# Experts of a mixed attention and expert layer: the gathered rows are turned by VectorE instead of TensorE, and the down product is accumulated in one bank region

## The reference, cut to what matters

```python
logits = jnp.einsum('bsd,de->bse', x, gate_w)            # 8 experts
affinity = jax.nn.softmax(logits, axis=-1)
gating, index = jax.lax.top_k(jnp.transpose(affinity, (0, 2, 1)), K)   # K = 256 rows of each batch
x_sel = x[b_idx, index]
g = jnp.einsum('bekd,edi->beki', x_sel, Wg)              # 256 -> 512
u = jnp.einsum('bekd,edi->beki', x_sel, Wu)
h = jax.nn.silu(g) * u
out = jnp.einsum('beki,eid->bekd', h, Wd)                # 512 -> 256
contrib = out * gating[..., None]
x_out = jnp.zeros_like(x).at[b_idx, index].add(contrib)
```

## Time and profile before

| | us |
|---|---|
| median of 3 runs | 1691.63 (1690.6 to 1692.41) |
| profiled execution, its own time | 1691.12 |
| its span, first to last instruction | 1689.2 |
| TensorE busy | 1643.0 (97%) |
| VectorE busy | 1046.5 (62%) |
| ScalarE busy | 1243.3 (74%) |
| POOL busy | 520.2 (31%) |

### The profile page before, as it was taken

The page is one execution under the profiler, slowest core; times in us unless marked ns, Lnnn a source line. Parts: engine busy times, 40 slices in busy tenths (PEclk is TensorE's granted clock), DMA queues, the critical chain, the costliest instruction groups (busy, mean ns, idle before and its releaser), DMA issues.

```text
span 1689.2 us, 27913 instructions
## 1 busy us (share of the span) xinstructions
PE 1643.0 (97%) x10616; PEld 926.4 (55%) x10616; DVE 1046.5 (62%) x2126; ACT 1243.3 (74%) x1544; POOL 520.2 (31%) x480
## 2 busy tenths in 40 slices
PE   6799999999999999999999999999999999999997
PEld 5234344344434434434434433368888888888886
DVE  9774566576575666567657668866555555555543
ACT  5798998998998899899899899954444444444443
POOL 3121121111211111112112100046666565656653
PEclk9799999999999999999999999999999999999999
DMA  5645753764684585476366366155443443534332
GB/s 186 162 104 118 155 134 69 182 136 108 149 173 110 122 177 133 107 161 160 95 151 162 86 146 130 40 162 112 86 95 65 94 95 64 100 63 96 67 56 33
DMA packets 113982, 196.00 MB, mean 116 GB/s; under 512 B 20896, under 2 KB 59680, under 8 KB 113696
## 3 DMA queue, kind: packets, MB, share of 16 engines
q1 hardware_dynamic: 83696, 143.01, 36.0%
q0 software_dynamic: 29040, 49.83, 15.3%
q10 hardware_dynamic: 1088, 1.05, 0.2%
HBM read 117.27 MB, written 76.55 MB: 115 GB/s over the span
## 4 chain that ended last, share of the span: by engine, by line
PE 87%; ACT 6%; DVE 3%; issue 2%; DMA 1%; POOL 1%; POOLq 0%; ACTq 0%; DVEq 0%
PE o_ps L1086 25%; PE score L1170 21%; PE score L1072 17%; ACT probs L854 6%; PE side L956 5%; PE score L1181 3%; PE side L966 3%; PE side L997 3%; PE o_ps L1181 2%; PE score L1183 2%; PE side L1181 2%; PE score L1157 2%; PE o_ps L1183 1%; PE side L1183 1%; PE side L936 1%
## 5 line engine op out<-in xcount | busy, mean ns | idle before, releaser
L854 ACT ACTIVATE probs<-score 128x1024 f32<-128x1024 f32 x1024 | 964.0, 1053 | 94.8 <-PE score L1072 88.8
L1086 PE MATMUL o_ps<-probs,v_ones 128*32 128x512 f32 x4096 | 514.7, 604 | 0.6
L1072 PE MATMUL score<-q_stack,k_stack 50*128 50x512 f32 x2048 | 377.1, 449 | 9.8 <-issue 4.4
L1072 PEld LDWEIGHTS score<-q_stack,k_stack 50*128 50x128 f32 x2048 | 166.4, 185 | 337.3 <-ACT probs L854 302.1
L752 POOL DMA_INDIRECT out<-probs,rot x128 | 212.3, 1659 | 191.7 <-DVE probs L1527 162.5
L833 ACT ACTIVATE probs<-score 128x512 f32<-128x512 f32 x128 | 76.6, 598 | 187.3 <-PE score L1170 187.3
L1086 PEld LDWEIGHTS o_ps<-probs,v_ones 128*32 128x32 f32 x4096 | 97.2, 108 | 210.8 <-issue 147.9
L1513 DVE TENSOR_TENSOR probs<-score,probs 128x512 f32<-128x512 f32 x128 | 88.5, 692 | 180.6 <-PE score L1170 176.3
L730 POOL TENSOR_TENSOR square<-qk 128x512 bf16<-128x512 f32 x56 | 71.0, 1298 | 345.3 <-DVE qk L1368 345.3
L741 POOL DMA_INDIRECT qk<-xn_rows,rot x128 | 135.1, 1055 | 38.3 <-issue 29.2
L1170 PE MATMUL score<-k_stack,zn_hi 128*128 128x512 f32 x512 | 140.1, 390 | 0.0
(11 more groups left out here) (271 smaller groups left out, 2348.3 us busy)
## 6 DMA issues: line engine op xcount, KB each, us to landing
q_parts<-parts SPq DMA_DIRECT2D x16, 1024.0 KB, 5.1
k_parts<-parts SPq DMA_DIRECT2D x16, 1024.0 KB, 8.4
q_stack<-q_parts SPq DMA_DIRECT2D x62, 256.0 KB, 6.2
k_stack<-k_parts SPq DMA_DIRECT2D x62, 256.0 KB, 7.9
q_stack<-q_parts SPq DMA_DIRECT2D x66, 128.0 KB, 6.2
k_stack<-k_parts SPq DMA_DIRECT2D x66, 128.0 KB, 6.7
o_sums<-o_sb SPq DMA_DIRECT2D x256, 32.0 KB
num<-o_sums SPq DMA_DIRECT2D x32, 256.0 KB
```

Of the source, the lines that this page charges most:

```text
L854: act.activation(probs[probs_of(b, s)][:, 2 * i:2 * i + 2, :], score[ring_of(b, p)][:, :, :], ACT.Exp, scale=SCALE).then_inc(exp_done, 1)
L1072: last = pe.matmul(score[ring_of(b, p)][:, w, :], k_stack[par][rows, i, kt * P:(kt + 1) * P], q_stack[par][rows, i, qh * HALF:(qh + 1) * H ...
L1086: last = pe.matmul(o_ps[j * KEYS_W:(j + 1) * KEYS_W, :], v_ones[par][:, kt, j, :], probs[probs_of(b, s)][:, j, :], start=kt == 0, stop=kt ...
```

## The change

1. Rows are turned on VectorE. `turn_rows(unit, a)` takes 32 of the 128 partitions of `xs` and writes, with four STREAM_TRANSPOSE of 32 partitions by 256 elements, one 32-row group of each tile to `x_turned`, a buffer in `cos_sb` that the experts don't use otherwise. Each of the four goes to another group of 32 partitions. Sixteen turn a unit: eight at the end of a unit for the unit after the next, four behind h(0) and four behind h(1) of the next unit. For unit 1, sixteen stand behind h(0) and h(1) of unit 0. TensorE keeps the eight transposes of the first unit alone (`turn_first`).
2. `turned` casts and subtracts 128x1024 at once, from SBUF, instead of twice 128x512 from PSUM.
3. `down` has three 256-wide matmuls for each t and f, all into one 256-column region; tiles 2 and 3 use the freed `xt_ps` banks instead of those of gate and up. For all four tiles first f = 0 and 1, then f = 2, then f = 3. ScalarE's scaling alone makes y; VectorE's (L1527) goes.
4. ScalarE's casts of weights stand before its scalings.
5. The four output projections run in units 1 and 2 between `gate_up` and `down`, instead of at the end of units 0 and 1, and VectorE's part of them stands before the last `low`.
6. POOL's gather waits until the rows of two units before are turned by VectorE (`rows_turned`), instead of by TensorE.

```diff
-        return (d_ps[0], d_ps[1], g_ps[(FC - 1) % 2], u_ps[(FC - 1) % 2])[t]
+        return (d_ps[0], d_ps[1], xt_ps[0], xt_ps[1])[t]
...
-    END_BANKS = {("wo", q): (q // 2, q % 2) for q in range(QUARTERS)}
+    END_BANKS = {("wo", q): (q // 2 + 1, q % 2 + 2) for q in range(QUARTERS)}
...
-            need(pool, xt_full, DC * (unit - 1))
+            if unit == 2:
+                pool.wait_ge(xt_full, DC)
+            elif unit > 2:
+                pool.wait_ge(rows_turned, unit - 2)
...
+            else:
+                act.wait_ge(rows_turned, unit)
+                act.wait_ge(up_full, FC * unit)
+                act.copy(x_hi[:, :, :], x_turned).then_inc(x_high, 1)
...
+            if bp < WEIGHTS and e + 1 < E:
+                high_weights(e + 1, bp)
             need(act, scattered[(bp - 2) % UNITS], ST * DMA * (e + (bp >= 2)))
             for t in range(ST):
                 act.wait_ge(down_full, ST * unit + t + 1)
-                act.activation(y[unit % 2][t], rows_ps(t)[:, D:2 * D], ACT.Copy,
+                act.activation(y[unit % 2][t], rows_ps(t)[:, 0:D], ACT.Copy,
...
-                    pe.matmul(rows_ps(t).rearrange("p (k n) -> p k n", k=2), h_hi[:, f, at], wd_both[k][:, :, f, :],
-                              start=f == 0, stop=False)
-                    last = pe.matmul(rows_ps(t)[:, 0:D], h_lo[f][:, at], we_hi[k][DOWN][:, f, :],
-                                     start=False, stop=f == FC - 1)
+                    for i, (ht, wt) in enumerate(((h_hi[:, f, at], we_hi), (h_lo[f][:, at], we_hi), (h_hi[:, f, at], we_lo))):
+                        last = pe.matmul(rows_ps(t)[:, 0:D], ht, wt[k][DOWN][:, f, :],
+                                         start=i == 0 and f == 0, stop=i == 2 and f == FC - 1)
...
             gate_up(unit)
-            if unit + 1 < E * UNITS:
-                turn(unit + 1)
+            for job in END_JOBS:
+                if END_BANKS[job][0] == unit:
+                    pe.wait_ge(y_scaled, ST * (unit - 1) + END_BANKS[job][1] + 1)
+                    run_job(end_jobs, job, None, NB - 1, rows_ps(END_BANKS[job][1]))
...
+        def turn_rows(unit, a):
+            if unit >= E * UNITS:
+                return
+            if a == 0:
+                dve.wait_ge(gathered[unit % 2], ST * DMA * (unit // 2 + 1))
+                dve.wait_ge(x_split, splits_of(unit - 1))
+            rows = slice(a * BLOCK, (a + 1) * BLOCK)
+            from_rows = xs[unit % 2][rows, :, :].rearrange("p t (c q n) -> p q c t n", c=DC, n=BLOCK)
+            to_cols = x_turned.rearrange("p c (t a k) -> p a c t k", t=ST, k=BLOCK)
+            for q in range(BLOCKS):
+                last = dve.transpose(to_cols[q * BLOCK:(q + 1) * BLOCK, a, :, :, :], from_rows[:, q, :, :, :])
+            if a == BLOCKS - 1:
+                last.then_inc(rows_turned, 1)
...
                 dve.tensor_tensor(h[f % 2], u_ps[f % 2], silu[f % 2], ALU.mult).then_inc(h_done, 1)
+                if unit == 0 and f < BLOCKS // 2:
+                    turn_rows(1, 2 * f)
+                    turn_rows(1, 2 * f + 1)
+                elif f < BLOCKS // 2:
+                    turn_rows(unit + 1, f + BLOCKS // 2)
                 if f > 0:
                     low(unit, f - 1)
...
             if bp < WEIGHTS and e + 1 < E:
                 low_weights(e + 1, bp)
+            turn_rows(unit + 2, 0)
+            turn_rows(unit + 2, 1)
```

## The result

| | before | after |
|---|---|---|
| median, us | 1691.63 (7 runs, 1690.41 to 1699.89) | 1677.72 (7 runs, 1676.23 to 1683.78) |
| profiled execution, its own time | 1691.12 | 1677.62 |
| its span | 1689.2 | 1675.8 |

The ratio is 0.9916, with a 95% interval of 0.9902 to 0.9931. The change makes the kernel faster, by some 14 us or 0.8%; I had said 22.6 (1668.5), with 1664 to 1685 as the range.

A forecast was written before the change was run, and what follows sets the result against it. TensorE's instruction list was taken as the bound. 28 units shorter by 0.954 us give 26.7 us, less 4.1 at the start is 22.6, so 1691.12 becomes 1668.5 us; range 1664 to 1685.

The forecast's parts named there:

- What bounds the kernel, and VectorE hidden: Steady units: TensorE's instruction list sets the time; VectorE's sixteen transposes cost nothing, with 1.0 us to spare.
- chain: VectorE's work in a steady unit with a weight, beside the transposes: 8.2 us, to which sixteen transposes are added.
- The price of the unseen form: A 32x256 STREAM_TRANSPOSE on VectorE, in no row of before: 0.45 us each without overlap, 7.2 us a unit.
- 48 x 0.114 = 5.47 us, against 5.64: TensorE's `down` in each unit: 48 256-wide matmuls at 0.114 us take 5.47 us, where before it took 5.64.
- the 26.7: Gain in us over 28 units, each 0.954 us shorter on TensorE without the eight transposes and with `down` at 5.47.
- The far end of 0.124: Slowest pace allowed for `down`, 0.124 us a 256-wide matmul: `down` 5.95 us, gain 0.47 a unit, 13 us.
- The start costs 4.1 us: First three units: transposes behind the last batch's work on VectorE make TensorE wait, so unit 3 starts 4.1 us later.
- "Cost nothing" of the casts of weights: ScalarE's casts of weights, moved ahead of its scalings, end at 14.6 us, before the first scaling is due: no cost.
- The gathers: POOL's rows for the unit three ahead land at 15.3 to 16.2 us, level with VectorE's need at 14.8 or 16.0.
- The slow `down` (1682): Rival: matmuls of `down` take 0.124 us, not 0.114, so 9 us less in all, 1682 us; chance 0.08.
- VectorE as the bound: Rival: transposes at 0.634 us make VectorE set steady units, 1718 us; chance 0.15, of which 0.12 slower.
- late gathers: Rival: POOL's scatters and gathers come late, 0.6 us a unit lost, between 1673 and 1685 us; chance 0.11.

The follow-up runs named there:

- experiments 3 and 4: The kernel after with two, and with four, further transposes a unit on VectorE into a spare buffer: 1679.43 us and 1695.55 us.
- experiment 8: The kernel after with each 32x256 transpose on VectorE cut into two of 32x128: 1677.92 us.
- Experiment 6: The kernel before with only `down` changed to three 256-wide matmuls and ScalarE's scaling alone, TensorE still transposing: 1693.48 us.
- experiment 7: The kernel after with the three products of `down` ordered high x high, high x low, low x high: 1675.34 us.
- experiment 9: The kernel after once more, unchanged, five executions: 1679.18 us, ratio to before 0.992.
- Experiment 2: The kernel after with the rows of units 1, 2 and 3 turned by TensorE instead of VectorE: 1667.97 us.
- experiment 5: The kernel after with rows of units 1 to 3 turned by TensorE and the silu table loaded early: 1665.50 us; run again, ratio to before 0.9845.
- Experiment 11: The kernel after with ScalarE's casts of weights put back behind its scalings: 1723.95 us.
- experiments 1 to 4 and 11: The first of these is the kernel after with the rows of unit 1 alone turned by TensorE: 1673.32 us; the others have their own lines.

## Why the prediction was right, and where it fell short

The mechanism was right and the time was in the range, but the gain was 14 us and not 22.6. Two terms of the sum were mis-sized, the pace of `down` (4.3 us) and the start (5.7 us); the 0.85 us by which the first `gate_up` came sooner is no merit of either kernel.

- **What bounds the kernel, and VectorE hidden: right.** TensorE's list bounded steady units before and does after. No wait of TensorE from 1200 to 1600 us; VectorE is busy 13.9 us of a unit (14 said); chain 8.35 us (8.2 said) and 1.05 us to spare (1.0 said), by experiments 3 and 4.
- **The price of the unseen form: right.** 0.45 us was put together from other rows; it is 0.436 long and 0.447 apart. That no overlap was counted is borne out by these rows and by the distance between pairs in experiment 8.
- **"48 x 0.114 = 5.47 us, against 5.64": mis-sized.** `down` takes 5.65, 0.1177 a matmul. I took the pace from one projection in unit 1. The same projection in unit 0, time line of PE of the kernel before, starts its pairs 0.235 apart, 0.1175 a matmul:

```profile
1132.97 0.40 PE L997 MATMUL score<-w_hi,at_lo 128*128 128x256 f32 x2
1133.21 0.40 PE L997 MATMUL score<-w_lo,at_hi 128*128 128x256 f32 x2
1133.44 0.40 PE L997 MATMUL score<-w_hi,at_hi 128*128 128x256 f32 x2
```

  Experiment 6 shows the narrow form as a loss of 0.095 us a unit by itself, and the transposes as a gain of 0.896. Together 0.801, 4.3 us less in all than the 26.7. The time lines of the kernel before have 32 such projections of 12 matmuls: behind their first pair 20 of them run at 0.118 and 12 at 0.113 to 0.115. So the form has two paces, I had read one of the quicker ones, and every steady `down` of after runs at the slower one. What sets the pace is open: the DMA share was 0.00 in both stretches, so traffic is not it, and the order of the products makes no difference to `down` (experiment 7). The far end of 0.124 had the late first matmul in it; without these 0.08 us it is 0.120.
- **"The start costs 4.1 us": right in place and mechanism, too small in size.** It cost 9.8 (7.5 in experiment 9's trace of the same kernel). Unit 0 took 23.29 us where 19.35 was worked out: h(0) started 7.2 us behind the first `gate_up`, not 3.7 as before, since the silu table was loaded late, and the transposes queued behind it pushed h(1) and the low parts. Experiment 7, with the early table, has 19.78: so the arithmetic of unit 0 held, and what failed in after is its first step, that h(0) is done when it was in the kernel before (1119.35). Unit 1 took 24.83 where 23.25 was worked out: TensorE's wait (3.5; 4.0 said) was followed by a lower clock, which the sum had at nothing and which cost some 1.7 us (an estimate from the windows at the end: 2.50 x 0.22 + 2.40 x 0.48). Unit 2 was met (21.93 against 21.8). TensorE waited 11.2 us in the rows of PE where some 9 was said. Experiment 2 shows the whole cost to hang on the transposes ahead of h: without them a table that is 4.6 us late costs 1.0 us (experiment 5), with them 3.5.
- **"Cost nothing" of the casts of weights: right only as a sum.** Experiment 11 shows that it is this move that keeps 16 transposes hidden: without it the units behind a weight lose 2.56 us and the kernel is slower than before by 31 us. I had put it among the edits of no weight, where it belonged among the conditions of the main one.
- **The gathers: right.** VectorE waits for them 1.0 us in all, in three places. The landing was level with the need, as said, and in experiment 8, which asks for them at a different time, it waited 5.0 us in ten places and the steady units are still 16.555.
- **The rivals.** The slow `down` (1682) is the one that partly came true, on the way from 0.114 to its 0.124. VectorE as the bound and late gathers did not.

## What to carry to other kernels

A pace read from one stretch is one sample: list every stretch of the same form before a term of 28 repeats is built on it. Here 20 of 32 would have shown the slower pace. Work that is hidden in the steady state isn't hidden in the first rounds, when the engine that takes it on is also finishing the stage before; leaving it where it was for units 1 to 3 got back 9.7 us here (experiment 2 beside after, one execution each), and with the table loaded early some 12. And when an engine in order is filled up, ask of every wait in its queue what now stands behind it: a step moved "for nothing" may be what carries the change.

## What the runs showed of the hardware

- **The clock after a wait.** Behind TensorE's 3.5 us wait in unit 1 the granted clock fell, for some 5 us. Windows of the kernel after (us; PE, PEld, DVE, ACT, POOL busy; clock; DMA; GB/s):

```profile
1143.00:1146.50 3.50, 0.07 (x1) 0.00 (x0) 3.40 (x8) 0.00 (x0) 2.92 (x4) 1.00 0.83 173
1146.50:1149.00 2.50, 2.43 (x8) 2.00 (x9) 2.41 (x6) 1.17 (x2) 1.89 (x3) 0.78 0.72 146
1149.00:1151.40 2.40, 2.40 (x7) 1.87 (x6) 2.30 (x6) 0.67 (x2) 1.58 (x2) 0.52 0.78 196
1151.50:1156.00 4.50, 4.50 (x30) 4.09 (x29) 3.27 (x7) 2.36 (x4) 0.00 (x0) 1.00 0.30 100
```

  0.52 is the lower of the two levels, 1.2 GHz, for nearly the whole stretch, and in it four 512-wide matmuls take 1.73 us instead of 1.07 (time line of PE, 1149.92). It fits the 1.6 us by which unit 1 was over. The length of a wait alone doesn't tell whether the clock falls: in after the waits of unit 0 (2.19, 1.13, 1.42 and 0.74 us) and unit 2 (2.23) have no fall behind them, in experiment 9, the same kernel, those of unit 0 (1.17, 1.42, 0.74) do and the 1.97 us of unit 1 doesn't. With no wait between 1116 and 1184 (experiment 5) the clock is 1.00 all through.
- **The table load.** It takes 1.28 us in every run, and the next activation starts 0.01 to 0.02 us behind its end. The Trainium skill, "ScalarE: Activation LUTs", section "What ACT_TABLE_LOAD costs", gives that duration and 1.38 us of draining besides; no such gap is seen here, neither ahead of the load nor behind it (experiment 5, where the cast ahead of it ends at 1111.49). What the runs do show is that it may start late: 1.7 us behind the first `gate_up` in before and experiments 6, 7 and 8, 5.3 in after, 3.0 in experiment 9 (the same kernel), and 2.8 to 6.1 in experiments 1 to 4 and 11. So it changes from one execution of a kernel to the next. What holds it back is open.
